# Token stage of an audio tower: the first depthwise tap on ScalarE, the latents' split one iteration earlier, and another order on four queues

## The chip, the cores and the metric

The kernel runs on one core of a Trainium2 chip. The metric is the device time of one execution in microseconds (us); the figure that is compared is the median over several runs.

## The reference

Only the first of three stages is touched: a token stage, then attention, then a mixture of low-rank experts. The token stage and the start of attention, cut to what matters:

```python
h = conv1d(x, conv_in_w, pad=3)                       # x (16, 64, 2048) -> (16, 128, 2048), 7 taps
h = gelu(groupnorm1(h, gn1_w, gn1_b))                 # one mean and variance per batch element
h = conv1d(h, dw_w, stride=2, pad=2, groups=128) + dw_b   # depthwise, 5 taps -> (16, 128, 1024)
h = gelu(groupnorm1(conv1d(h, pw_w), gn2_w, gn2_b))   # pointwise 128x128
t = layernorm(h)
q_c = rmsnorm(t @ w_qa, g_qa)                         # 384 latents per token
kv = t @ w_kva; k_c = rmsnorm(kv[..., :128], g_kva)   # 128 latents, and 64 rotary columns
k_rope = rope(kv[..., 128:])
```

Everything is float32 in the reference. The kernel splits an operand into a high and a low float16 part and adds three products (high x high, high x low, low x high).

## The kernel before, in words

`token_phase` works on one batch element b at a time, 128 channels on the partitions. `pipeline` (L65) calls each engine's own `body(i, p, ok)` with i from -1 to 20; `ok(lag)` says whether batch element i - lag exists, so that one iteration works on several elements at different steps. AHEAD = -1 is the loading and splitting of x, 0 the first conv, MID = 1 GELU 1, the depthwise taps and the pointwise matmul, HID = 2 GELU 2 and the layer norm's statistics, PROJ = 3 the normalised hidden row, its turning and the projection, TAIL = 4 the latents' scales and high parts, LOW = 5 their low parts. Each engine has one queue and goes through its body in the order written; semaphores join them. A full iteration is one in which all of these exist.

What each queue does in an iteration, in order:

- **TensorE**: conv chunk 0 (12 matmuls, L561), the averaging of the statistics over the partitions (`stat_ps`, L599), conv chunks 1 to 3, `project` (48 matmuls, L582 and L583, which wait for the turned `ht`), `pointwise` (L570, waits for the five taps, `dw_step`).
- **VectorE**: copy of the averages to `s` (L490); low part of the hidden row `hid2` (L412); low parts of the latents, `latents_low`; `take_latents` (L453 to L458); statistics of y, chunk 0; `add_rotary`; chunk 1; the five `tap`s (L437 for the first, L441 for the other four); `bn_stats` and `bn_aggr` of resid (L513, L519); `reciprocal` of the latents' scales `rinv` (L523, waits for GpSimd's `rms_step`); statistics of y, chunks 2 and 3; `mean_and_square` of y (ready: `st1_ready`); statistics of the pointwise result (L536) and its `mean_and_square` (`st2_ready`).
- **ScalarE**: `hid` (L271, waits for the layer norm, `ln_step`) and its high part (L275); copies of conv results to y (L261), with the high part of the next x (`x_high`, L255) behind the first; GELU 1 (L288, waits for `gn_step`); GELU 2 (L296); the latents' high parts (L305 to L307, wait for `rinv_done`); the two squares with their sums (L314, L317, wait for the projection).
- **GpSimd**: `group_norms` (eleven small instructions, L347 to L357, waits for `s`); `x_low`, the low part of the next x (L335, 128x2054); `latent_scales` (seven small instructions, L366 to L372, waits for the squares); `layer_norm` (eight, L382 to L389, waits for `bn3_step`). In a profile the last instruction of each chain stands on its last line.
- **SP**: the turning of `hid2` (L202), the turning of the latents and of kc (L206, L209), the load of the x after next (L195, waits for both parts of x).

The lines on which order and waits hang, on VectorE:

```python
                if ok(MID):
                    for k in range(DW_TAPS):
                        tap(i - MID, k)
                ...
                if ok(TAIL):
                    b = i - TAIL
                    dve.wait_ge(rms_step, b * RMS_STEPS + RMS_STEPS)
                    dve.reciprocal(rinv[:, :], nrm[:, :]).then_inc(rinv_done, 1)
```

and on GpSimd, whose code is the same before and after:

```python
                if ok(MID) or ok(HID):
                    group_norms(i)
                if ok(AHEAD) and i >= 0:
                    x_low(i - AHEAD)
                if ok(TAIL):
                    latent_scales(i - TAIL)
                if ok(HID):
                    layer_norm(i - HID)
```

Of the kernel before, what the change touches and what calls it, by code (L numbers as in the profile page):

```python
# [18 lines left out]
ALU = mybir.AluOpType  # L19
# [5 lines left out]
XW = T + 2 * PAD  # L25
PAIRS = (TAPS + 1) // 2
D = T // 2
# [81 lines left out]
def token_phase(nc, keep, raw_loaded, x_d, wc_d, wqk_d, pw_d, rows_d, params_d, consts_d, heads_d):  # L109

    AHEAD, MID, HID, PROJ, TAIL, LOW = -1, 1, 2, 3, 4, 5
    LAST = B - 1
    with ExitStack() as ctx:
# [64 lines left out]
        lags = list(range(AHEAD, LOW + 1))  # L180
# [9 lines left out]
        def _(sp):  # L190
# [6 lines left out]
            def body(i, p, ok):  # L197
# [5 lines left out]
                if ok(LOW):  # L203
                    b = i - LOW
# [6 lines left out]
                if ok(-2) and i >= -1:  # L211
                    sp.wait_ge(x_hi, i + 2)
                    sp.wait_ge(x_lo, i + 2)
                    load(i + 2, 0, XW, x_loaded)
# [17 lines left out]
            pipeline(sp, body, -1, lags, LOW)  # L232
# [4 lines left out]
        def _(act):  # L237
# [27 lines left out]

            def body(i, p, ok):
                if ok(PROJ):
# [17 lines left out]
                if ok(MID):  # L285
# [23 lines left out]
                if ok(PROJ):  # L309
                    b = i - PROJ  # L310
                    act.wait_ge(proj_done, b + 1)
                    need(act, rms_step, b * RMS_STEPS, B * RMS_STEPS)
                    need(act, ss_done, b * 2, 2 * B)
                    act.activation(junk[:, :], q_ps[:, 0:QR], ACT.Square, scale=UN * QR ** -0.5,  # L314
                                   accum_out=ss[:, 0:1]).then_inc(ss_done, 1)
                    act.wait_ge(ss_done, b * 2 + 1)
                    act.activation(junk[:, 0:KVR], kv_ps[:, 0:KVR], ACT.Square, scale=UN * KVR ** -0.5,  # L317
                                   accum_out=ss[:, 1:2]).then_inc(ss_done, 1)

            act.wait_ge(zeroed, ZEROED)  # L320
            pipeline(act, body, -1, lags, LOW)

        @block.gpsimd
        def _(pool):
# [79 lines left out]
            pipeline(pool, body, -1, lags, LOW)  # L404

        @block.vector
        def _(dve):
# [24 lines left out]
            def tap(b, k):  # L432

                if k == 0:
                    dve.wait_ge(gelu1_done, b + 1)
                    need(dve, pw_done, b * 2, 2 * B)
# [992 lines left out]
```

## Time and profile before

| what | value |
|---|---|
| median of three runs | 2041.67 us (2041.35 to 2043.67) |
| profiled execution | 2044.69 us |
| its span | 2042.9 us, mean granted TensorE clock 0.969 |
| TensorE matmul, share of the span | 93% |
| VectorE | 65% |
| ScalarE | 38% |
| GpSimd | 15% |

The time of a run is that of the whole launch; the span is what the profiler saw between the first and the last instruction, so the profiled execution has 1.8 us around its span. The profiled execution is a run of its own and need not lie at the median. In the rows further below, times are us from the span's start, PE is TensorE, DVE VectorE, ACT ScalarE, POOL GpSimd, SPq the DMA queue of SP. Buffer numbers are left out of names (g for g1, y for y1_0 and y1_1, c for c12, lat for lat2). `x4` is a count of like instructions merged into one row, whose length is then that of all. What stands in brackets is how long the engine sat idle before, and who ended that.

### The profile page before, as it was taken

The numbers are of one execution on the slowest core, as the hardware profiler recorded it, in microseconds if no ns is written. First come the engines' busy times: TensorE is split into PE (matmuls) and PEld (weight loads), VectorE is DVE, ScalarE is ACT, GpSimd is POOL, SyncE is SP. The second block draws the span as 40 slices with busy tenths as digits, with TensorE's granted clock in tenths as the row PEclk, the third lists the DMA queues.
The fourth block names the chain that finished last, engine by engine and source line by source line (L and its number), as shares of the span: only waits on it lengthen the run. The fifth ranks groups of instructions, "written<-read, shape, count | busy, mean of one in ns | idle before, by whom it ended". The sixth has DMA issues, their size and how long they took to land. (4 is left out here: it accounts for less than half of the span.)

```text
span 2042.9 us, 32412 instructions
## 1 busy us (share of the span) xinstructions
PE 1892.5 (93%) x11538; PEld 1029.6 (50%) x11538; DVE 1321.2 (65%) x2742; ACT 773.2 (38%) x2020; POOL 308.4 (15%) x596
## 2 busy tenths in 40 slices
PE   4898898559999999999999999999999999859999
PEld 2344444335555555555555555555555555425554
DVE  4678777436666666666666666666666666555554
ACT  3454554233333334433333433333343333332221
POOL 2376675300000000000000000000000000033332
PEclk9899999679999999999999999999999999979999
DMA  5244342332222322232222222223222222243332
GB/s 143 52 86 96 81 95 65 76 91 51 58 58 59 76 56 53 58 76 59 58 58 55 73 58 58 58 58 75 55 55 58 40 39 39 39 138 80 80 82 73
DMA packets 305609, 138.87 MB, mean 68 GB/s; under 512 B 295088, under 2 KB 295344, under 8 KB 303408
## 3 DMA queue, kind: packets, MB, share of 16 engines
q1 hardware_dynamic: 301136, 108.35, 24.8%
q10 hardware_dynamic: 4320, 28.51, 4.0%
q8 instruction: 92, 1.51, 0.3%
q14 instruction: 61, 0.50, 0.1%
HBM read 56.07 MB, written 8.39 MB: 32 GB/s over the span
## 5 line engine op out<-in xcount | busy, mean ns | idle before, releaser
L1031 PE MATMUL out_ps<-m_h,ot_h 128*128 128x512 f16 x1024 | 389.4, 380 | 1.7 <-DVE ot_l L835 1.7
L1032 PE MATMUL out_ps<-m_l,ot_h 128*128 128x512 f16 x1024 | 389.0, 380 | 0.0
L1033 PE MATMUL out_ps<-m_h,ot_l 128*128 128x512 f16 x1024 | 388.9, 380 | 0.0
L756 ACT ACTIVATE qp_h<-qp_ps 128x512 f16<-128x512 f32 x126 | 75.3, 597 | 492.6 <-PE qp_ps L966 492.6
L812 ACT ACTIVATE prob<-s_ps,nmx 128x128 f32<-128x128 f32 x512 | 181.3, 366 | 207.3 <-DVE nmx L905 207.3
L885 DVE SCALAR_TENSOR_TENSOR resid<-out_ps,resid 128x512 f32<-128x512 f32 x256 | 176.1, 688 | 97.1 <-PE out_ps L1033 97.1
L835 DVE SCALAR_TENSOR_TENSOR qp_l<-qp_ps,qp_h 128x512 f16<-128x512 f32 x126 | 87.2, 692 | 234.5 <-ACT qp_h L756 234.5
L1221 POOL MEMSET fpower<- 128x1 f32 x1 | 0.1, 99 | 1392.4 <-POOLq L674 1392.4
L966 PE MATMUL qp_ps<-lat,wp_h 128*128 128x512 f16 x756 | 205.6, 381 | 0.0
L1033 PEld LDWEIGHTS out_ps<-m_h,ot_l 128*128 128x128 f16 x1024 | 100.4, 98 | 121.6 <-issue 1.4
L1031 PEld LDWEIGHTS out_ps<-m_h,ot_h 128*128 128x128 f16 x1024 | 100.5, 98 | 110.5 <-DVE ot_l L835 2.7
L1032 PEld LDWEIGHTS out_ps<-m_l,ot_h 128*128 128x128 f16 x1024 | 100.5, 98 | 107.7 <-issue 0.8
L982 PE MATMUL rope_ps<-wr_h,lat 128*128 128x256 f16 x768 | 127.8, 276 | 0.0
L966 PEld LDWEIGHTS qp_ps<-lat,wp_h 128*128 128x128 f16 x756 | 74.4, 98 | 90.9 <-issue 2.3
L835 DVE SCALAR_TENSOR_TENSOR halves<-prob,halves 128x512 f16<-128x512 f32 x128 | 88.6, 692 | 46.5 <-ACT halves L756 46.5
L756 ACT ACTIVATE halves<-prob 128x512 f16<-128x512 f32 x128 | 80.8, 631 | 84.5 <-DVE prob L911 84.5
L812 ACT ACTIVATION_READ_ACCUMULATOR prob<-s_ps,nmx 128x1 f32 x512 | 103.8, 203 | 0.0
L966 PE MATMUL qp_ps<-lat,wp_l 128*128 128x512 f16 x378 | 102.6, 381 | 0.0
L835 DVE SCALAR_TENSOR_TENSOR ot_l<-av_ps,ot_h 128x512 f16<-128x512 f32 x128 | 88.4, 690 | 21.3 <-ACT ot_h L756 17.8
L582 PE MATMUL q_ps<-wqk_h,ht 128*128 128x384 f16 x256 | 78.7, 342 | 24.5 <-DMA ht<-hid_hl 24.5
L1334 PE MATMUL fout<-wb_h,fht_h 128*128 128x512 f16 x256 | 97.3, 380 | 0.0
L1334 PE MATMUL fout<-wb_l,fht_h 128*128 128x512 f16 x256 | 97.3, 380 | 0.0
(217 smaller groups left out, 3861.3 us busy)
## 6 DMA issues: line engine op xcount, KB each, us to landing
wide<-heads_in ACTq DMA_DIRECT2D x30, 928.0 KB, 4.7
wide<-x_in SPq DMA_DIRECT2D x30, 512.0 KB, 6.5
tower_out<-result SPq DMA_DIRECT2D x16, 512.0 KB, 2.6
stage<-wb_in SPq DMA_DIRECT2D x8, 512.0 KB, 8.3
resid<-wqk_in SPq DMA_DIRECT2D x1, 2304.0 KB, 11.6
zt<-z SPq DMA_TRANSPOSE x128, 2.4
turned<-halves SPq DMA_TRANSPOSE x128, 3.0
wide<-heads_in SPq DMA_DIRECT2D x2, 928.0 KB, 4.6
```

What stands on the lines that cost most here:

```text
L582: pe.matmul(q_ps[:, 0:QR], lhs, w[:, k, 0:QR], start=first, stop=end)
L756: act.activation(out, src, ACT.Copy, scale=scale).then_inc(done, 1)
L812: act.activation(prob[:, h, :], s_ps[:, h * P:(h + 1) * P], ACT.Exp, bias=nmx[:, h:h + 1], scale=EXP_SCALE, accum_out=rsum[:, h:h + 1]).th ...
L835: dve.scalar_tensor_tensor(out=out, in0=src, scalar=scale, in1=high, op0=ALU.mult, op1=ALU.subtract).then_inc(done, 1)
L885: dve.scalar_tensor_tensor(out=resid[:, at], in0=out_ps[hf][:, :], scalar=1.0 / (O_S * M_S), in1=resid[:, at], op0=ALU.mult, op1=ALU.add). ...
L966: last = pe.matmul(bank[:, :], w[:, bass.ds(side, 1), k, j, :].rearrange("p a n -> p (a n)"), q[:, k, bass.ds(tok, CHUNK)], start=n == 0, ...
L982: last = pe.matmul(rope_ps[:, 0:HEADS * RD], q[:, k, bass.ds(tok + j * P, P)], w[:, bass.ds(side, 1), k, :].rearrange("p a n -> p (a n)"), ...
L1031: pe.matmul(out_ps[hf][:, :], ot_h[:, h, :], m_h[:, at], start=h == 0, stop=False)
L1032: pe.matmul(out_ps[hf][:, :], ot_h[:, h, :], m_l[:, at], start=False, stop=False)
L1033: last = pe.matmul(out_ps[hf][:, :], ot_l[:, h, :], m_h[:, at], start=False, stop=h == HEADS - 1)
L1221: pool.memset(power[:, :], -0.5).then_inc(powered, 1)
L1334: pe.matmul(out_ps[p][hf][:, :], h[p][:, k, :], w[:, k, hf * CHUNK:(hf + 1) * CHUNK], start=k == 0 and n == 0, stop=False)
```

## The change

- Tap 0 of the depthwise conv, with its bias, moves from VectorE (`tensor_scalar`) to ScalarE (`activation` Identity with scale and bias), right behind GELU 1. Taps 1 to 4 stay.
- `reciprocal` moves from behind bn3 to between taps 2 and 3.
- LOW is gone: the latents' low parts are made at the end of the iteration in which their high parts are made. The stage has one iteration less.
- On VectorE the low part of hid stands behind the statistics of y's chunk 0 (for i < 16; from then on in front of `take_latents`); the statistics of y's chunks 2 and 3 stand in front of those of resid, and the statistics of the pointwise result in front of y's `mean_and_square`.
- On ScalarE the squares of the last iterations (batch elements 13 to 15) stand behind hid of the iteration after.
- On SP the load of x stands in front of the latents' turnings.
- The low part of x stays on GpSimd, in its place.

The diff, cut to its core:

```diff
-    AHEAD, MID, HID, PROJ, TAIL, LOW = -1, 1, 2, 3, 4, 5
+    AHEAD, MID, HID, PROJ, TAIL = -1, 1, 2, 3, 4
...
@@ ScalarE @@
+                if ok(TAIL) and i - TAIL + PROJ >= B:
+                    squares(i - TAIL)
                 if i == 0:
...
                     act.activation(g1[:, DW_PAD:DW_PAD + T], y1[1 - p][:, :], ACT.Gelu, bias=c12[:, 1:2],
                                    scale=c12[:, 0:1]).then_inc(gelu1_done, 1)
+                    b = i - MID
+                    act.wait_ge(gelu1_done, b + 1)
+                    need(act, pw_done, b * 2, 2 * B)
+                    act.activation(dw[:, :], g1[:, 0:2 * D:2], ACT.Identity, bias=params[:, 5:6],
+                                   scale=params[:, 0:1]).then_inc(dw_step, 1)
...
+                if ok(PROJ) and i < B:
+                    squares(i - PROJ)
@@ VectorE @@
-                if ok(PROJ):
-                    b = i - PROJ
-                    dve.wait_ge(hid_hi, b + 1)
-                    need(dve, hid_turned, b * 16, B * 16)
-                    low(hid2[:, D:2 * D], hid[:, :], LN_S, hid2[:, 0:D], hid_lo)
-                if ok(LOW):
-                    latents_low(i - LOW)
+                if ok(PROJ) and i >= B:
+                    hid_low(i - PROJ)
                 if ok(TAIL):
                     take_latents(i - TAIL)
                 if ok(0):
                     stats1(i, p, 0)
+                if ok(PROJ) and i < B:
+                    hid_low(i - PROJ)
                 if ok(TAIL):
                     add_rotary(i - TAIL)
                 if ok(0):
                     stats1(i, p, 1)
-                if ok(MID):
-                    for k in range(DW_TAPS):
+                for k in range(1, DW_TAPS):
+                    if ok(MID):
                         tap(i - MID, k)
+                    if ok(TAIL) and k == 2:
+                        dve.wait_ge(rms_step, (i - TAIL) * RMS_STEPS + RMS_STEPS)
+                        dve.reciprocal(rinv[:, :], nrm[:, :]).then_inc(rinv_done, 1)
+                if ok(0):
+                    stats1(i, p, 2)
+                    stats1(i, p, 3)
                 if ok(HID):
...
+                if ok(TAIL):
+                    latents_low(i - TAIL)
@@ SP @@
+                if ok(-2) and i >= -1:
+                    sp.wait_ge(x_hi, i + 2)
+                    sp.wait_ge(x_lo, i + 2)
+                    load(i + 2, 0, XW, x_loaded)
-                if ok(LOW):
-                    b = i - LOW
+                if ok(TAIL):
+                    b = i - TAIL
```

VectorE's queue in a full iteration before, from the first tap to the copy of `s` (the names are the buffers'; bn3 and st3 belong to the layer norm):

```order
L437 TENSOR_SCALAR dw<-g1,params 128x1024 [waits pw_done,gelu1_done]
L441 SCALAR_TENSOR_TENSOR dw<-g1,params,dw 128x1024 [waits dw_step] x4
L513 BN_STATS bn3<-resid 128x6 [waits gelu2_done]
L513 BN_STATS bn3<-resid 128x6
L519 BN_AGGR st3<-bn3 128x2 [waits bn3_step,ln_step]
L523 RECIPROCAL rinv<-nrm 128x2 [waits rms_step]
L421 BN_STATS bn1<-y1_0 128x6 [waits y1_copied] x2
L428 BN_AGGR st<-bn1 128x2 [waits bn1_done,stat_done]
L429 SCALAR_TENSOR_TENSOR st<-st 128x1 [waits st1_ready]
L536 BN_STATS bn2<-pw_ps0 128x6 [waits pw_done]
L536 BN_STATS bn2<-pw_ps1 128x6 [waits pw_done]
```

The same place after the change (its lines are numbered by the changed file):

```order
L442 SCALAR_TENSOR_TENSOR dw<-g1,params,dw 128x1024 [waits dw_step] x2
L514 RECIPROCAL rinv<-nrm 128x2 [waits rms_step]
L442 SCALAR_TENSOR_TENSOR dw<-g1,params,dw 128x1024 [waits dw_step] x2
L429 BN_STATS bn1<-y1_0 128x6 [waits y1_copied] x2
L522 BN_STATS bn3<-resid 128x6 [waits gelu2_done]
L522 BN_STATS bn3<-resid 128x6
L528 BN_AGGR st3<-bn3 128x2 [waits bn3_step,ln_step]
L533 BN_STATS bn2<-pw_ps0 128x6 [waits pw_done]
L533 BN_STATS bn2<-pw_ps1 128x6 [waits pw_done]
L436 BN_AGGR st<-bn1 128x2 [waits bn1_done,stat_done]
L437 SCALAR_TENSOR_TENSOR st<-st 128x1 [waits st1_ready]
```

The first tap has left the queue, the reciprocal with its wait for GpSimd stands in front of half of the taps, and the statistics are in another order.

ScalarE's queue after the change, from the high part of the next x to the copy behind the second GELU's:

```order
L254 ACTIVATE wide1<-wide0 128x2054 [waits conv_done,x_loaded]
L260 ACTIVATE y1_1<-conv_ps2 128x512 [waits conv_done]
L299 ACTIVATE g1<-y1_0,c12 128x2048 [waits dw_step,gn_step]
L304 ACTIVATE dw<-g1,params 128x1024 [waits pw_done,gelu1_done]
L260 ACTIVATE y1_1<-conv_ps0 128x512 [waits conv_done]
L312 ACTIVATE resid<-pw_ps0,c12 128x512 [waits gn_step]
L312 ACTIVATE resid<-pw_ps1,c12 128x512
L260 ACTIVATE y1_1<-conv_ps1 128x512 [waits conv_done]
```

Its fourth row is new; before, the copy of y followed GELU 1 at once.

## Rows read from the trace of the kernel before

**Rows 1.** Busy time of each engine in two stretches of the token stage.
```profile
core 0: us, PE busy (x) PEld busy (x) DVE busy (x) ACT busy (x) POOL busy (x), PEclk, DMA share, GB/s
99.69:337.56 237.87, 210.67 (x1124) 109.68 (x1122) 185.98 (x338) 126.35 (x189) 166.36 (x298) 0.97 0.41 87
337.56:420.70 83.14, 43.10 (x239) 25.84 (x236) 40.79 (x97) 26.62 (x50) 30.08 (x92) 0.75 0.29 61
```

**Rows 2.** Timeline of VectorE, one full iteration: start, length, engine, line, instruction, idle before.
```profile
236.88 2.16 DVE L437 TENSOR_SCALAR dw<-g,params 128x1024 f32<-128x1024 f32 x1 [1.99 <-ACT g L288]
239.07 5.25 DVE L441 SCALAR_TENSOR_TENSOR dw<-g,params,dw 128x1024 f32<-128x1024 f32 x4
244.23 1.28 DVE L513 BATCH_NORM_STATS2 bn<-resid 128x6 f32<-128x512 f32 x2
...
245.81 0.11 DVE L523 RECIPROCAL rinv<-nrm 128x2 f32<-128x2 f32 x1
...
250.14 0.16 DVE L490 COPY s<-stat_ps 128x4 f32<-128x4 f32 x1 [0.49 <-PE stat_ps L599]
...
252.72 0.61 DVE L412 SCALAR_TENSOR_TENSOR lat<-q_g,rinv,lat 128x384 f16<-128x384 f32 x1
```

**Rows 3.** Timeline of GpSimd, the same iteration.
```profile
229.12 0.19 POOL L347 TENSOR_TENSOR msq<-s 128x2 f32<-128x2 f32 x1 [1.31 <-DVE s L490]
...
234.67 3.82 POOL L335 TENSOR_TENSOR x_l<-wide 128x2054 f16<-128x2054 f32 x1
...
239.30 1.63 POOL L367 TENSOR_TENSOR ry<-rv,half 128x2 f32<-128x2 f32 x1 [0.18 <-POOL rv L366]
...
246.11 0.23 POOL L382 TENSOR_SCALAR lv<-st 128x1 f32<-128x1 f32 x1 [0.98 <-DVE st L519]
...
248.99 0.19 POOL L389 TENSOR_TENSOR lc<-lm,ly 128x1 f32<-128x1 f32 x1 [0.18 <-POOL ly L388]
250.51 0.20 POOL L347 TENSOR_TENSOR msq<-s 128x2 f32<-128x2 f32 x1 [1.33 <-DVE s L490]
```

**Rows 4.** Timeline of ScalarE, the same iteration.
```profile
234.74 2.10 ACT L288 ACTIVATE g<-y,c 128x2048 f32<-128x2048 f32 x1 [1.79 <-POOL c L357]
```

**Rows 5.** Timeline of all engines, the second iteration.
```profile
39.18 4.07 POOL L335 TENSOR_TENSOR x_l<-wide 128x2054 f16<-128x2054 f32 x1 [3.56 <-ACT wide L255]
...
40.57 3.90 DVE L412 SCALAR_TENSOR_TENSOR wqk_l<-resid,wqk_h 128x1152 f16<-128x1152 f32 x1 [0.36 <-ACT wqk_h L242]
...
44.39 0.80 DVE L437 TENSOR_SCALAR dw<-g,params 128x1024 f32<-128x1024 f32 x1
```

**Rows 6.** Timeline of GpSimd, the latents' scales of the last batch.
```profile
411.24 0.21 POOL L366 TENSOR_SCALAR rv<-ss 128x2 f32<-128x2 f32 x1 [13.00 <-ACT junk L317]
411.63 0.71 POOL L367 TENSOR_TENSOR ry<-rv,half 128x2 f32<-128x2 f32 x1 [0.18 <-POOL rv L366]
...
414.05 0.19 POOL L372 TENSOR_SCALAR nrm<-nrm 128x2 f32<-128x2 f32 x1 [0.20 <-POOL nrm L371]
```

**Rows 7.** Timeline of TensorE, the same iteration and one of four with a slow pointwise matmul.
```profile
235.48 1.02 PE L561 MATMUL conv_ps<-x_l,wc_h 128*128 128x512 f16 x4
...
244.37 1.98 PE L570 MATMUL pw_ps<-dw,pw 128*128 128x512 f32 x4 [1.90 <-DVE dw L441]
...
330.76 3.35 PE L570 MATMUL pw_ps<-dw,pw 128*128 128x512 f32 x4 [1.98 <-DVE dw L441]
```

**Rows 8.** Timeline of all engines, the drained end of the stage.
```profile
388.19 0.19 POOL L389 TENSOR_TENSOR lc<-lm,ly 128x1 f32<-128x1 f32 x1 [0.18 <-POOL ly L388]
...
392.74 0.49 ACT L314 ACTIVATE junk<-q_ps 128x384 f16<-128x384 f32 x1 [6.10 <-PE kv_ps L583]
...
393.62 1.23 ACT L271 ACTIVATE hid<-resid,lc,ly 128x1024 f32<-128x1024 f32 x1
...
397.22 1.86 SPq L202 DMA_TRANSPOSE ht<-hid_hl  x1
...
401.72 0.48 PE L582 MATMUL q_ps<-wqk_h,ht 128*128 128x384 f16 x1 [9.02 <-DMA ht<-hid_hl]
```

More of the change, by code:

```diff
@@ L179, in token_phase @@
         HEAD = 2 * CHUNK + 8
-        lags = list(range(AHEAD, LOW + 1))
+        lags = list(range(AHEAD, TAIL + 1))
         block = ctx.enter_context(nc.Block())
@@ L264, in copy_y1, with squares @@
                     weights_high("wqk", QUARTERS[c])
+            def squares(b):
+                act.wait_ge(proj_done, b + 1)
+                need(act, rms_step, b * RMS_STEPS, B * RMS_STEPS)
+                need(act, ss_done, b * 2, 2 * B)
+                act.activation(junk[:, :], q_ps[:, 0:QR], ACT.Square, scale=UN * QR ** -0.5,
+                               accum_out=ss[:, 0:1]).then_inc(ss_done, 1)
+                act.wait_ge(ss_done, b * 2 + 1)
+                act.activation(junk[:, 0:KVR], kv_ps[:, 0:KVR], ACT.Square, scale=UN * KVR ** -0.5,
+                               accum_out=ss[:, 1:2]).then_inc(ss_done, 1)
             def body(i, p, ok):
@@ L432, in tap, with hid_low @@
             def tap(b, k):
-                if k == 0:
-                    dve.wait_ge(gelu1_done, b + 1)
-                    need(dve, pw_done, b * 2, 2 * B)
-                    dve.tensor_scalar(dw[:, :], g1[:, 0:2 * D:2], params[:, 0:1], params[:, 5:6],
-                                      ALU.mult, ALU.add).then_inc(dw_step, 1)
-                else:
-                    dve.wait_ge(dw_step, b * DW_TAPS + k)
-                    dve.scalar_tensor_tensor(out=dw[:, :], in0=g1[:, k:k + 2 * D - 1:2],
-                                             scalar=params[:, k:k + 1], in1=dw[:, :],
-                                             op0=ALU.mult, op1=ALU.add).then_inc(dw_step, 1)
+                dve.wait_ge(dw_step, b * DW_TAPS + k)
+                dve.scalar_tensor_tensor(out=dw[:, :], in0=g1[:, k:k + 2 * D - 1:2],
+                                         scalar=params[:, k:k + 1], in1=dw[:, :],
+                                         op0=ALU.mult, op1=ALU.add).then_inc(dw_step, 1)
+            def hid_low(b):
+                dve.wait_ge(hid_hi, b + 1)
+                need(dve, hid_turned, b * 16, B * 16)
+                low(hid2[:, D:2 * D], hid[:, :], LN_S, hid2[:, 0:D], hid_lo)
             def take_latents(b):
@@ L519, in body @@
                     dve.bn_aggr(st3[:, :], bn3[:, :, :]).then_inc(bn3_step, 1)
-                if ok(TAIL):
-                    b = i - TAIL
-                    dve.wait_ge(rms_step, b * RMS_STEPS + RMS_STEPS)
-                    dve.reciprocal(rinv[:, :], nrm[:, :]).then_inc(rinv_done, 1)
+                if ok(MID):
+                    b = i - MID
+                    for hf in range(2):
+                        dve.wait_ge(pw_done, b * 2 + (hf + 1))
+                        dve.bn_stats(bn2[:, hf, :], pw_ps[hf][:, :]).then_inc(bn2_done, 1)
                 if ok(0):
-                    stats1(i, p, 2)
-                    stats1(i, p, 3)
                     waits = [(bn1_done, i * 4 + 4)]
@@ L532, in body @@
                 if ok(MID):
-                    b = i - MID
-                    for hf in range(2):
-                        dve.wait_ge(pw_done, b * 2 + (hf + 1))
-                        dve.bn_stats(bn2[:, hf, :], pw_ps[hf][:, :]).then_inc(bn2_done, 1)
                     wait_apart(dve, dve_passed, (bn2_done, b * 2 + 2), (stat_done, i))
                     mean_and_square(st2_ready, b, st[:, 2:4], bn2[:, :, :])
+                if ok(TAIL):
+                    latents_low(i - TAIL)
             dve.wait_ge(zeroed, ZEROED)
             dve.wait_ge(w_loaded["params"], 16)
-            pipeline(dve, body, -1, lags, LOW)
+            pipeline(dve, body, -1, lags, TAIL)
         @block.tensor
```

22 lines of the change are left out of this document (4 added, 18 removed).

## Prediction

> **What bounds the kernel now.** I read the windows first [rows 1]. The token stage runs to 420.70 us of a span of 2042.9, and only that stage is touched. Its full iterations (i = 4 to 14, the 11 that load, convolve, scale and project at once) take 237.87 us, 21.62 each. VectorE is busy 185.98 of them and TensorE 210.67 (its granted clock 0.97), so neither is full by itself: something hands on. To see what, I followed one iteration through the timelines of VectorE and GpSimd [rows 2, 3], from GpSimd's first group-norm instruction at 229.12 to the next at 250.51: 21.39 us, in three pieces.
>
> - A, 9.37 us: the small group-norm instructions to 234.67, then the low half of x, 3.82 us, to 238.49. ScalarE's GELU starts when the group norm is done and ends at 236.84 [rows 4].
> - B, 5.83 us: tap 0 on VectorE starts at 236.88 but takes 2.16 us, to 239.04, though it needs 0.80 when GpSimd is idle; then four taps of 1.28 to 244.32.
> - C, 6.19 us: `bn_stats`, the moments of both group norms (249.65), the averaging matmul, the copy of `s` at 250.14, and GpSimd's start.
>
> All of it is one chain, without slack. GpSimd's other work hangs beside it: the seven instructions of the latents' scales after the low half, of which VectorE's reciprocal at 245.81 did not wait, and the layer norm, 246.11 to 249.18.
>
> The other thing to see is that GpSimd and VectorE hold each other up. A split of wqk on VectorE that started at 40.57 beside the low half of x (39.18 to 43.25) took 3.90 us and ended at 44.47 [rows 5]: it stood until 43.25 and ended 1.22 later. The other way round, GpSimd's pow at 239.30 took 1.63 us and ended at 240.93, 0.57 after tap 1 had ended [rows 3]; with VectorE idle it takes 0.71, and the seven instructions of the scales 3.00 (411.24 to 414.24) [rows 6].
>
> **The change, part by part.**
>
> *Tap 0 on ScalarE.* VectorE loses 2.19 us (236.88 to 239.07) an iteration. ScalarE gains one Identity of 128x1024; nearest rows are 1.23 for the same form without a stride (hid, at 393.62) [rows 8] and 2.10 for 2048 elements [rows 4]; I take 1.25 and keep 2.10 as the end. GELU ends 7.72 into the cycle, so tap 0 is done at 9.0, before the low half of x (9.3). Tap 1 reads two operands from SBUF as the wqk split did, so it cannot go before the low half is over: it ends 1.20 after that where tap 1 ended 240.36, 1.87 after it. The tap is worth 0.65 us, not 2.19, and ScalarE's price is covered by the low half; at 2.10 it would miss by 0.5. The low half itself does not move: its code on GpSimd is the same, and so are its order and its length (3.82 to 4.1).
>
> The Trainium skill ("SBUF — State Buffer", SBUF: two separate sides) says that whichever of the two engines starts first keeps the pair for its whole instruction and the other is blocked fully. By that rule tap 1 would begin from nothing at the end of the low half and end 1.28 after it, where the wqk row shows 1.22; the sum would be 1 us higher.
>
> *The reciprocal between taps 2 and 3.* This is the term that decides. `rinv` is wanted 4.4 us earlier than before, and the reciprocal is a wait in the middle of VectorE's queue: taps 3 and 4, the pointwise matmul, all `bn_stats` after them, the layer norm and the next group norm stand behind it. GpSimd computes the scales after the low half. Counted from the end of the low half: its first small instruction is held by tap 1 to 1.20, the pow by tap 2 to 2.48 and ends 0.57 later, at 3.05; VectorE now stands, so the five left go unheld in 1.90 (pow's end at 412.34 to 414.24 [rows 6]), to 4.95; the reciprocal with its handing over 0.20; taps 3 and 4 2.56. B becomes **7.71 instead of 5.83**, +1.88 us, with a wait of about 2.4 us that was not there. Bounds: +0.0 if tap 1 and 2 do not hold GpSimd (3.1 for the scales, 0.2, 2.56), +3.2 if one more hold of a tap's length (1.28) falls into the five.
>
> *Stats 2, 3 before bn3, latents' low parts at the end.* The two `bn_stats` of y go ahead of those of resid, 1.2 us, so the layer norm's input is ready 2.8 after the last tap instead of 1.6. GpSimd then needs 0.2 + 3.08 (246.11 to 249.18) + 0.2 [rows 3]: the next group norm can start at 6.2. Other path: the moments, 5.33 after the last tap now, come some 0.4 sooner (no reciprocal, and waits on the instruction before are filled by others), at 4.9; then the low parts of the latents (three instructions, the first 0.61 at 252.72; about 1.1 together [rows 2]) stand ahead of the copy of `s`, to 6.0, and 0.36 of handing over: 6.35. They also hold the layer norm's last instructions, 0 to 1.0; I take 0.2. C is 6.4, +0.2. Where they stood before, behind the copy, they cost nothing, and the space left there is idle now.
>
> *Low part of hid behind the first stats.* As long as hid's own making (1.23 for 128x1024 [rows 8]), it holds one of GpSimd's group-norm instructions, as before, only later in their chain. A stays at 9.37; bounds −1.2 (no hold) and +0.3.
>
> *Queues.* The transpose of hid is issued some 2 us later in the cycle, since ScalarE makes hid when the layer norm is done and its low part comes after the first stats. From issue (397.22) to the projection's first matmul (401.72) is 4.5 us [rows 8], so the projection starts near 9.0, 1.6 us after the last conv. It takes 6.0 (from the last conv's end at 236.50 to 1.90 before the pointwise matmul at 244.37 [rows 7]) and ends at 15.0; the pointwise matmul waits for the last tap at 17.1. Covered. If that cover of 2.1 us went, each iteration would pay what is over. SP now loads x ahead of the latents' transposes: it waits for the low half anyway, and the landing has a whole iteration. Free.
>
> *First and last iterations.* i = 2 and 3 have no reciprocal: they gain 0.65 each, −1.3. At the end, ScalarE stood idle 6.10 us for the projection of b = 14 and only then made hid of b = 15 (393.62), whose layer norm was done at 388.38 [rows 8]. Now the squares come behind it: up to 5.2 us. But from i = 15 each iteration hands on lateness: +0.6 for i = 15 (tap 0 there 1.25 against 0.80), +2.0 for i = 16 (the layer norm is done at the cycle's start instead of 1.3 before, the latents' low parts stand ahead of the copy), and bn3 of b = 15 now waits for the reciprocal, +1.3. Net −1.3.
>
> **Sum.** Per full iteration 1.87 + 0.2 = +2.07, 11 times: +22.8. The mean of 21.62 stands 0.23 above the iteration that I followed: in 4 of the 11 TensorE's clock is down at the pointwise matmul (3.35 us for it at 330.76, 1.98 at 244.37 [rows 7]) and the averaging matmul is late. In the longer C about half of these 2.5 us is covered: −1.2. With −1.3 and −1.3: **+19.0 us**. The profiled execution, 2044.69, would be 2063.7. It stood 3.0 above the median of the runs, 2041.67, and a median is what is forecast: **2060.7 us**, slower by 0.9%. What lies within 0.2% (4 us) a measurement of this kernel can't tell from no change.
>
> **The rivals.**
>
> *1. GpSimd is not held.* Its small instructions slip in beside taps 1 and 2. The point that decides is the end of the scales: at 3.1 us after the low half the reciprocal costs nothing, since tap 2 ends at 2.5 and the gain of 0.65 pays the rest. The loop stays at 21.6, and the ends give −1.3 and, with nothing handed on late, −5.2: 2035.2, faster. For it: VectorE idles longer in the new order, and at 411.24 the same chain ran unheld [rows 6]. Against: rows 3, in every full iteration. 0.10. If the last part gives less, about 2039: no change, 0.05.
> The Trainium skill ("Perfetto Trace Analysis", Optimizing Scalar/DVE Operations) says that where VectorE is saturated, giving some work to ScalarE can make sense. Here VectorE is at 78%, so the rule's condition is not met; read as 2.19 us less on one engine and 1.25 more on another, it would give −0.94 an iteration, some −10 us with nothing else, 2031.
>
> *2. TensorE's clock stays low.* There are now two gaps a cycle (1.6 and 1.9 us). Should the clock be down at 1.2 GHz for half of the projection, that takes 3.0 more and ends at 18.0, 0.9 after the last tap, and the pointwise matmul 1.4 more; with the first conv behind it slow in part, the averaging matmul comes some 1.5 later than C allows: 11 x 1.5 more, 2077. For it: a granted clock of 0.75 in the drained part, where TensorE waits [rows 1]. Against: 0.97 in the full iterations, with one gap of 1.90 already in each. 0.08.
>
> *3. The wait is longer than forecast*, since the reciprocal stands behind one more hold (B +3.2): 2075; or part of it is hidden (B +1.0): 2051. Both are the forecast's own mechanism, within its 0.77. That the change would do nothing is not a rival: the program orders differ in every iteration.
>
> **How the numbers follow.** 0.77 for the forecast (2051 to 2069), 0.10 for rival 1 faster, 0.05 no change, 0.08 for rival 2. The range 2048 to 2069 leaves out rival 1, rival 2 and a small part of the forecast's upper end. Faster 0.11, same 0.05, slower 0.84.
>
> **What would show it.** In the changed profile: full iterations of 23.4 to 23.8 us between copies of `s`; a new wait "VectorE reciprocal on GpSimd nrm", 2.0 to 2.8 us long, 11 times; tap 0 on ScalarE 1.2 to 1.3; tap 1 of about 1.3 to 1.6 that ends 1.2 after the low half; the scales' chain 4.9 long; no ScalarE idle before hid of b = 15. Wrong would be: a reciprocal without a wait (then rival 1), tap 1 that runs beside the low half, or TensorE with a clock under 0.9 in 100 to 350 us (rival 2).

## Result and profile after

The changed kernel takes **2054.99 us** (median of 4 runs, 2054.52 to 2056.96). Beside it the kernel before took 2042.31 (4 runs); the ratio is 1.0065, with a 95% interval from 1.0053 to 1.0077. It is slower by 12.7 us. Forecast were 2060.7 and a range of 2048 to 2069: right in sign, inside the range, 5.7 us too high; as a difference, 12.7 us where 19.0 were forecast. The profiled execution took 2054.52 us, 1.8 more than its span.

The page of the changed kernel, its head:

```profile
span 2052.7 us, 32412 instructions
## 1 busy us (share of the span) xinstructions
PE 1895.9 (92%) x11538; PEld 1031.7 (50%) x11538; DVE 1288.9 (63%) x2726; ACT 795.2 (39%) x2036; POOL 287.4 (14%) x596
```

The windows, cut 0.36 us behind the same copies of `s` as [rows 1] (the 11 full iterations, then the drained end):

```profile
core 0: us, PE busy (x) PEld busy (x) DVE busy (x) ACT busy (x) POOL busy (x), PEclk, DMA share, GB/s
94.77:348.90 254.13, 215.76 (x1126) 112.39 (x1124) 162.08 (x332) 141.06 (x198) 147.65 (x298) 0.96 0.38 78
348.90:431.00 82.10, 43.28 (x237) 25.92 (x235) 37.87 (x91) 31.28 (x53) 27.27 (x94) 0.76 0.33 73
```

The full iterations take 254.13 us instead of 237.87, although VectorE is busy 24 us less (162.08 against 185.98). It lost work and gained idle time. The timeline of VectorE, the same full iteration as [rows 2]:

```profile
237.57 1.23 DVE L420 SCALAR_TENSOR_TENSOR hid_hl<-hid,hid_hl 128x1024 f16<-128x1024 f32 x1
...
242.74 2.68 DVE L442 SCALAR_TENSOR_TENSOR dw<-g,params,dw 128x1024 f32<-128x1024 f32 x2 [2.78 <-ACT dw L304]
247.93 0.17 DVE L514 RECIPROCAL rinv<-nrm 128x2 f32<-128x2 f32 x1 [2.51 <-POOL nrm L380]
248.01 2.58 DVE L442 SCALAR_TENSOR_TENSOR dw<-g,params,dw 128x1024 f32<-128x1024 f32 x2
250.51 1.28 DVE L429 BATCH_NORM_STATS2 bn<-y 128x6 f32<-128x512 f32 x2
...
256.24 0.15 DVE L496 COPY s<-stat_ps 128x4 f32<-128x4 f32 x1
```

GpSimd over the same time, which answers to [rows 3]:

```profile
234.12 0.19 POOL L355 TENSOR_TENSOR msq<-s 128x2 f32<-128x2 f32 x1
...
237.91 0.95 POOL L364 TENSOR_TENSOR msq<-s,c 128x2 f32<-128x2 f32 x1 [0.18 <-POOL c L363]
...
239.19 3.82 POOL L343 TENSOR_TENSOR x_l<-wide 128x2054 f16<-128x2054 f32 x1
243.10 1.07 POOL L374 TENSOR_SCALAR rv<-ss 128x2 f32<-128x2 f32 x1
244.35 1.64 POOL L375 TENSOR_TENSOR ry<-rv,half 128x2 f32<-128x2 f32 x1 [0.18 <-POOL rv L374]
246.17 0.20 POOL L376 TENSOR_TENSOR rv<-rv,ry 128x2 f32<-128x2 f32 x1 [0.18 <-POOL ry L375]
...
247.70 0.19 POOL L380 TENSOR_SCALAR nrm<-nrm 128x2 f32<-128x2 f32 x1 [0.19 <-POOL nrm L379]
...
255.32 0.59 POOL L394 TENSOR_TENSOR lt<-lt,lv 128x1 f32<-128x1 f32 x1 [0.18 <-POOL lt L393]
...
256.93 0.19 POOL L397 TENSOR_TENSOR lc<-lm,ly 128x1 f32<-128x1 f32 x1 [0.18 <-POOL ly L396]
257.15 0.19 POOL L355 TENSOR_TENSOR msq<-s 128x2 f32<-128x2 f32 x1
```

Taps 1 and 2 run until 245.42 and hold the first two instructions of the scales (1.07 and 1.64 us instead of 0.21 and 0.71). Then VectorE stands for 2.51 us until the last of the seven, at 247.89, releases the reciprocal. The last rows show a second thing: the next group norm, at 257.15, starts with no idle time right behind the layer norm, while the copy of `s` had ended at 256.39; before, GpSimd stood there for 1.33 us and waited for the copy [rows 3]. The waits of the token stage show the reciprocal's as a new line (14 times; the 11 in the full iterations are 2.50 to 2.52 us each), and the tap's new place (engine, what it waits for, total, times, longest):

```profile
DVE dw L442 <- ACT dw L304: 47.9, 16, 5.3
DVE rinv L514 <- POOL nrm L380: 35.1, 14, 3.7
```

From the same views come the pieces of one iteration, as the prediction cuts it: A from GpSimd's first group-norm instruction to the end of the low half of x, B from there to the end of the last tap, C to the next first instruction. The last column is the distance between copies of `s`, the mean of the 11 full iterations. The first three columns and their sum are of one iteration in the middle of the stage. The kernels below the row of the forecast are told of in the next section.

| kernel | A | B | C | sum | mean of 11 |
|---|---|---|---|---|---|
| before | 9.37 | 5.83 | 6.19 | 21.39 | 21.62 |
| changed | 8.89 | 7.58 | 6.56 | 23.03 | 23.10 |
| forecast | 9.37 | 7.71 | 6.4 | 23.48 | 23.58 |
| tap on ScalarE alone | 9.35 | 5.05 | 6.19 | 20.59 | 20.69 |
| reciprocal back | 8.89 | 5.04 | 6.25 | 20.18 | 20.48 |
| reciprocal behind tap 4 | 8.89 | 5.05 | 7.95 | 21.89 | 21.99 |
| reciprocal behind tap 3 | 8.89 | 6.70 | 6.55 | 22.14 | 22.22 |
| tap 0 back | 8.88 | 7.47 | 6.55 | 22.90 | 23.00 |
| low parts behind the copy | 8.95 | 7.57 | 6.40 | 22.92 | 22.99 |
| best | 9.31 | 5.03 | 5.66 | 20.00 | 20.06 |

One iteration is not the mean: the low half of x takes 3.8 and 4.1 us by turns, and the holds in A and the end of C differ between iterations. As means of the 11, A, B and C are 9.37, 5.83 and 6.43 before and 8.99, 7.58 and 6.54 in the changed kernel. So the 1.48 us an iteration are made of −0.37, +1.74 and +0.11 (rounded).

### The profile page after: what moved, and what is told of

It reads as the page before. It is cut to its first block and busy times, and to the rows that moved or that the text cites. A ratio compares the mean times of both kernels' runs of the same rounds, so it can differ in the third digit from the quotient of the medians.

```text
span 2052.7 us, 32412 instructions
## 1 busy us (share of the span) xinstructions
PE 1895.9 (92%) x11538; PEld 1031.7 (50%) x11538; DVE 1288.9 (63%) x2726; ACT 795.2 (39%) x2036; POOL 287.4 (14%) x596
## 5 line engine op out<-in xcount | busy, mean ns | idle before, releaser
L588 PE MATMUL q_ps<-wqk_h,ht 128*128 128x384 f16 x256 | 85.3, 365 | 55.1 <-DMA ht<-hid_hl 55.1
L442 DVE SCALAR_TENSOR_TENSOR dw<-g,params,dw 128x1024 f32<-128x1024 f32 x64 | 84.5, 1320 | 49.2 <-ACT dw L304 47.9
```

The lines of the kernel that those rows point to most:

```text
L442: dve.scalar_tensor_tensor(out=dw[:, :], in0=g1[:, k:k + 2 * D - 1:2], scalar=params[:, k:k + 1], in1=dw[:, :], op0=ALU.mult, op1=ALU.add) ...
L588: pe.matmul(q_ps[:, 0:QR], lhs, w[:, k, 0:QR], start=first, stop=end)
```

## Experiments

The theory: the reciprocal in the middle of the taps makes VectorE wait for GpSimd's scales, and that costs some 2.6 us in each of 11 iterations, while the rest of the change gains. The rivals: something else of the change costs (the low parts ahead of the copy, the order of statistics, the squares), or the tap on ScalarE does. Each ratio is to runs of the kernel before on the same chip.

**The reciprocal goes back behind bn3**, all else as changed.

```diff
-                    if ok(TAIL) and k == 2:
-                        dve.wait_ge(rms_step, (i - TAIL) * RMS_STEPS + RMS_STEPS)
-                        dve.reciprocal(rinv[:, :], nrm[:, :]).then_inc(rinv_done, 1)
...
                     dve.bn_aggr(st3[:, :], bn3[:, :, :]).then_inc(bn3_step, 1)
+                if ok(TAIL):
+                    dve.wait_ge(rms_step, (i - TAIL) * RMS_STEPS + RMS_STEPS)
+                    dve.reciprocal(rinv[:, :], nrm[:, :]).then_inc(rinv_done, 1)
```

> The changed kernel with the reciprocal moved back behind the statistics of resid; all else as changed. Theory W (the wait in the middle of the taps is what costs): the wait of 2.5 us on nrm goes, GpSimd's chain is held by all taps again, and a full cycle falls from 23.1 to 20.6 to 21.0 us (9.0 to the end of the low half of x, 5.0 of taps, 6.6 behind them, some loss to the projection, which now ends after the last tap): 11 cycles of -2.2, so some 2031, ratio to the kernel before 0.993 to 0.997. Rival O (the new order of the statistics and of the latents' low parts is what costs): the time stays at 2050 to 2055.

Measured: 2025.98 us, ratio 0.9930 (0.9917 to 0.9944), faster than the 2031 that were expected. The reversal is worth 2.62 us an iteration, and the rest of the change is a gain of 14 us. Its VectorE and GpSimd:

```profile
227.47 5.32 DVE L442 SCALAR_TENSOR_TENSOR dw<-g,params,dw 128x1024 f32<-128x1024 f32 x4 [2.78 <-ACT dw L304]
...
231.71 1.14 POOL L377 TENSOR_TENSOR rt<-rv,ry 128x2 f32<-128x2 f32 x1 [0.18 <-POOL rv L376]
...
233.81 0.19 POOL L380 TENSOR_SCALAR nrm<-nrm 128x2 f32<-128x2 f32 x1 [0.20 <-POOL nrm L379]
...
235.48 0.11 DVE L528 RECIPROCAL rinv<-nrm 128x2 f32<-128x2 f32 x1
```

The four taps run on end, the scales are held longer (they end 6.25 us after the low half instead of 4.88), and nobody waits: the reciprocal comes 1.5 us later still. Ten of the 11 iterations take 20.34 in the mean. In the last one the projection falls on a stretch at the lower clock, takes 7.70 us instead of 6.04, and the iteration takes 21.83.

**The reciprocal alone**, put between taps 2 and 3 of the kernel before (tap 0 stays on VectorE).

```diff
+                    if ok(TAIL) and k == 2:
+                        dve.wait_ge(rms_step, (i - TAIL) * RMS_STEPS + RMS_STEPS)
+                        dve.reciprocal(rinv[:, :], nrm[:, :]).then_inc(rinv_done, 1)
```

> The kernel before with one edit: the reciprocal and its wait between taps 2 and 3. Theory W: GpSimd's first three small instructions are held by taps 0, 1 and 2, the rest runs unheld; reciprocal 4.85 us after the low half of x, last tap at 7.45 instead of 5.83: +1.6 us in each of 11 cycles, +15 to +20 in all, 2057 to 2062, ratio 1.007 to 1.010. Rival O: at most +3.

Measured: 2062.04 us, ratio 1.0112 (1.0097 to 1.0128), at the upper end of what was expected. The wait is 1.61 us and the last tap ends 7.47 us after the low half, where 7.45 was thought, but the distance between copies of `s` is 23.63, 2.01 more than before: 1.64 in B, and 0.47 in C, which was not forecast (A takes 0.11 back). From 214 us on it alternates (25.21, then 22.70 from 239.25 to 261.95). The timeline of VectorE and TensorE in a long one:

```profile
228.86 0.17 DVE L511 RECIPROCAL rinv<-nrm 128x2 f32<-128x2 f32 x1 [1.61 <-POOL nrm L372]
...
231.59 3.78 PE L569 MATMUL pw_ps<-dw,pw 128*128 128x512 f32 x4 [3.91 <-DVE dw L441]
...
239.25 0.16 DVE L490 COPY s<-stat_ps 128x4 f32<-128x4 f32 x1 [2.46 <-PE stat_ps L598]
```

Here the projection is over early, TensorE stands for 3.91 us before the pointwise matmul, and this then takes 3.78 us, about twice the 1.98 of [rows 7]; the copy waits 2.46 for the averages instead of 0.49. The granted clock over the full iterations is 0.93, against 0.97 before. The wait of VectorE is handed on as a second price at TensorE: C is 8.09 in this iteration and 6.13 in the next, where the four matmuls take 1.98. In the changed kernel that part is covered, as point 5 below shows.

**The tap alone**: tap 0 on ScalarE in the kernel before.

```diff
+                    act.activation(dw[:, :], g1[:, 0:2 * D:2], ACT.Identity, bias=params[:, 5:6],
+                                   scale=params[:, 0:1]).then_inc(dw_step, 1)
...
-                    for k in range(DW_TAPS):
+                    for k in range(1, DW_TAPS):
```

> The kernel before with one edit: tap 0 on ScalarE behind GELU 1. Theory L (the low half of x on GpSimd holds the first tap whichever it is): tap 1 ends 1.14 us after the low half instead of 1.87, so -0.7 us a cycle, 11 to 13 cycles, +0.4 in the two iterations without a low half: -7 to -9 in all, 2033 to 2035, ratio 0.995 to 0.9965. Rival (ScalarE's tap is simply taken off VectorE, 2.19 less and 1.30 more in the chain, no hold): -0.9 a cycle and tap 1 starting before the low half ends: -10 or more; rival 2 (nothing gained, the tap was covered): 0.

Measured: 2030.49 us, ratio 0.9952 (0.9939 to 0.9966), 0.93 us an iteration. B is 0.79 shorter. C is 0.24 shorter in the mean: TensorE's clock is 1.00 in this stretch, and no iteration has a late averaging matmul. A is 0.09 longer in the mean:

```profile
95.90:323.50 227.60, 204.86 (x1124) 107.82 (x1123) 162.66 (x328) 140.30 (x199) 162.98 (x297) 1.00 0.43 91
```

**The latents' low parts behind the copy**, one iteration later, as before the change. SP's old order (load of x last) came back with it, so the two are not told apart.

```diff
-                if ok(TAIL):
-                    latents_low(i - TAIL)
...
+                if ok(LOW):
+                    latents_low(i - LOW)
                 if ok(TAIL):
                     take_latents(i - TAIL)
```

> The changed kernel with the latents' low parts one iteration later again, behind the copy of s, and SP's order as before. Theory (they stand ahead of the copy and hold the layer norm's last instructions): the piece behind the taps falls from 6.56 to about 6.2 us, -0.35 a cycle, -3 to -5 in all against the changed kernel, 2050 to 2052, ratio 1.004 to 1.005. Rival O: this is where the loss is, -10 or more. Rival 3: nothing, since the layer norm itself sets the next group norm.

Measured: 2050.97 us, ratio 1.0054 (1.0040 to 1.0068). Its interval overlaps that of the changed kernel, so the time alone does not settle it. The trace gives 0.11 us an iteration (22.99 against 23.10), a third of the 0.35 that were expected: small, and not where the 12.7 us come from. The low parts hold GpSimd in either place: ahead of the copy it is the layer norm's fifth and sixth instruction (0.59 and 0.27 us), behind it the seventh and eighth (0.50 and 0.29), 0.19 each unheld.

**The changed kernel again**, on the chip of the two runs that follow and of the best version.

> The changed kernel once more, on the same chip as the three runs beside it, as their yardstick. Ratio to the kernel before 1.0053 to 1.0077, as measured first.

Measured: 2055.44 us, ratio 1.0064 (1.0050 to 1.0077).

**The scales ahead of the low half of x** on GpSimd, so that the reciprocal finds them ready.

```diff
-                if ok(AHEAD) and i >= 0:
-                    x_low(i - AHEAD)
                 if ok(TAIL):
                     latent_scales(i - TAIL)
+                if ok(AHEAD) and i >= 0:
+                    x_low(i - AHEAD)
```

> The changed kernel with the latents' scales ahead of the low half of x on GpSimd. Theory G (GpSimd's share of the cycle, group norm 5.1 + low half 3.9 + scales, sets when taps 3 and 4 can run, and the wait on nrm is only where it shows): the scales run unheld in 3.0 and the reciprocal waits no longer, but the low half then ends 12.0 us into the cycle and holds tap 1 until then; last tap at 17.0 instead of 16.5, a cycle of 23.4 to 23.7: 2058 to 2062, ratio 1.008 to 1.010. Theory W' (the reciprocal's wait alone costs): about the time of the run with the reciprocal moved back, 2026 to 2030.

Measured: 2062.76 us, ratio 1.0108 (1.0091 to 1.0125), just above what theory G gave. The seven instructions take 3.01 us unheld and the reciprocal has no wait, but the low half ends 12.35 after the iteration's start, and no tap gets past it:

```profile
247.83 3.82 POOL L343 TENSOR_TENSOR x_l<-wide 128x2054 f16<-128x2054 f32 x1
248.15 5.90 DVE L442 SCALAR_TENSOR_TENSOR dw<-g,params,dw 128x1024 f32<-128x1024 f32 x2 [3.13 <-ACT dw L304]
253.97 0.16 DVE L514 RECIPROCAL rinv<-nrm 128x2 f32<-128x2 f32 x1
```

Two taps take 5.90 instead of 2.56. The two lock each other out, in whichever order: a reciprocal so early has to be paid for once, as a wait or as a hold.

**The squares of batch elements 13 to 15 at their old place.**

```diff
-                if ok(TAIL) and i - TAIL + PROJ >= B:
-                    squares(i - TAIL)
...
-                if ok(PROJ) and i < B:
+                if ok(PROJ):
```

> The changed kernel with the two squares of batch elements 13 to 15 at their old place, at the end of the iteration. Theory D (moving them gave the drained end back what the rest of the change costs there): the end of the stage is 2 to 5 us longer, ratio 1.0075 to 1.009 where the changed kernel has 1.0065. Rival: nothing, because the projection of b = 15 waits for that of b = 14 and for its transposes anyway.

Measured: 2060.10 us, ratio 1.0088 (1.0074 to 1.0102). hid of element 15 starts at 408.11 instead of 404.07, and attention's first matmul at 434.71 instead of 431.44. The move gains 3.3 us by the trace, and 4.7 by the medians (2055.44 for the changed kernel beside it).

**The reciprocal behind tap 3, and behind tap 4**, ahead of all statistics (`k == 3` and `k == 4` in place of `k == 2`).

> The changed kernel with the reciprocal one tap later, between taps 3 and 4. Theory H (the scales' instructions on GpSimd are held by each tap that runs, and the reciprocal stalls the rest): tap 3 ends 3.8 us after the low half of x and holds the instruction behind the pow until then; the three behind that run unheld and end near 5.3; the reciprocal 5.5, the last tap 6.8 after the low half instead of 7.6. 0.8 us an iteration less than the changed kernel, cycle 22.3, 11 x 0.8 = 9 us: 2044 to 2048, 1.001 to 1.004 of the kernel before. Theory F (only the place of bn3 and of the low parts costs): no difference from the changed kernel, 2055.

> The changed kernel with the reciprocal right behind tap 4, ahead of all statistics. Theory H: the four taps end 5.1 us after the low half; the chain of scales has one more held instruction, ends near 6.2, and the reciprocal waits 1.1 and ends at 6.4; the statistics behind it start there instead of at 7.6. Cycle 21.9, 11 x 1.2 = 13 us less than the changed kernel: 2040 to 2044, 0.999 to 1.002 of the kernel before; slower than the same kernel with the reciprocal behind bn3 (2026 in an earlier run, 0.993), where the wait is gone. Theory F: 2055.

Measured: behind tap 3 2046.78 us, ratio 1.0018 (1.0008 to 1.0028); behind tap 4 2043.01, ratio 1.0001 (0.9991 to 1.0011). Both lie in what the theory gave, with 10 runs each. First behind tap 3, then behind tap 4:

```profile
243.92 0.17 DVE L514 RECIPROCAL rinv<-nrm 128x2 f32<-128x2 f32 x1 [1.62 <-POOL nrm L380]
244.01 1.27 DVE L442 SCALAR_TENSOR_TENSOR dw<-g,params,dw 128x1024 f32<-128x1024 f32 x1
```

```profile
237.14 5.32 DVE L442 SCALAR_TENSOR_TENSOR dw<-g,params,dw 128x1024 f32<-128x1024 f32 x4 [2.79 <-ACT dw L304]
...
243.70 0.17 DVE L514 RECIPROCAL rinv<-nrm 128x2 f32<-128x2 f32 x1 [1.24 <-POOL nrm L380]
```

With nothing changed but the place of one instruction of 0.17 us, the wait goes 2.51, 1.62, 1.24, none, and the iteration 23.10, 22.22, 21.99, 20.48. Each tap that goes ahead holds GpSimd once more (0.62 instead of 0.20 us, then 1.14 instead of 0.20), so a tap of 1.28 us buys 0.9 and then 0.4 of wait. The last step, behind the statistics, takes off 1.5: the rest of the wait, the reciprocal and its handing over.

**Tap 0 back on VectorE**, the reciprocal where the change puts it (the tap as in the kernel before, the rest as changed).

> The changed kernel with tap 0 back on VectorE; the reciprocal stays between taps 2 and 3. Theory H (GpSimd's scales are held by the taps, and the wait sets the cycle): with tap 0 back the taps end and so the holds come 0.65 us later, so the scales and the reciprocal come 0.65 later, but the wait of the reciprocal stays near 1.6 to 2.5 us; 11 x 0.65 is +7 us on the changed kernel: 2062 to 2066, 1.009 to 1.012 of the kernel before. Theory F (the scales have their own time, 5 us after the low half, whatever VectorE does): the wait only gets shorter by 0.65, and the time is that of the changed kernel, 2055.

Measured: 2053.63 us, ratio 1.0073 (1.0056 to 1.0090). Theory H, my own, fell here, and F held: what gained 9 us in the kernel before gains nothing that can be measured in the changed one. VectorE and GpSimd from the end of the low half, 244.53:

```profile
242.91 2.16 DVE L438 TENSOR_SCALAR dw<-g,params 128x1024 f32<-128x1024 f32 x1 [1.44 <-ACT g L299]
...
244.61 0.54 POOL L369 TENSOR_SCALAR rv<-ss 128x2 f32<-128x2 f32 x1
...
245.33 1.64 POOL L370 TENSOR_TENSOR ry<-rv,half 128x2 f32<-128x2 f32 x1 [0.18 <-POOL rv L369]
...
249.10 0.19 POOL L375 TENSOR_SCALAR nrm<-nrm 128x2 f32<-128x2 f32 x1 [0.20 <-POOL nrm L374]
249.33 0.17 DVE L517 RECIPROCAL rinv<-nrm 128x2 f32<-128x2 f32 x1 [1.61 <-POOL nrm L375]
```

The scales end 4.76 us after the low half here, 4.88 in the changed kernel. The taps lie some 0.7 later, so the first instruction of the scales is held less (0.54 instead of 1.07), and one behind the pow a little more (L371, 0.62 instead of 0.20). The last tap hangs on the scales, so the earlier tap only makes the wait longer (2.51 instead of 1.61).

**Next to no low half of x**: 8 of its 2054 columns are computed and the rest is left out, so that GpSimd has no long instruction.

```diff
+            pool.memset(x_l[1][:, :], 0.0)
...
-                pool.tensor_tensor(x_l[p][:, :], x_f[:, :], x_h[p][:, :], ALU.subtract).then_inc(x_lo, 1)
+                pool.tensor_tensor(x_l[p][:, 0:8], x_f[:, 0:8], x_h[p][:, 0:8], ALU.subtract).then_inc(x_lo, 1)
```

> The changed kernel in which the low half of x is computed for 8 of its 2054 columns only and the rest of that tile holds zeros or stale halves; all other instructions are there. Theory H: with the low half away the scales run from 5.1 us after the cycle's start and are done near 8.5, before tap 2 ends; the reciprocal loses its wait, tap 1 follows tap 0 at 9.0 unheld, the last tap ends near 14.0 instead of 16.5. The cycle goes from 23.1 to about 20.5 us, unless the projection, which then ends last, holds TensorE; 2025 to 2030, 0.991 to 0.994 of the kernel before. Rival (the wait comes of the latents' squares or of VectorE's order, not of GpSimd's load): cycle over 22.5 us and a time over 2045.

Measured: 2021.85 us, ratio 0.9911 (0.9895 to 0.9928), below what was expected; the distance between copies is 20.41. GpSimd's last instruction of the scales and VectorE:

```profile
223.22 0.19 POOL L381 TENSOR_SCALAR nrm<-nrm 128x2 f32<-128x2 f32 x1 [0.20 <-POOL nrm L380]
...
223.68 2.61 DVE L443 SCALAR_TENSOR_TENSOR dw<-g,params,dw 128x1024 f32<-128x1024 f32 x2 [3.13 <-ACT dw L304]
...
226.20 0.16 DVE L515 RECIPROCAL rinv<-nrm 128x2 f32<-128x2 f32 x1
```

The scales are done before tap 1 starts, and the reciprocal between taps 2 and 3 costs nothing. What it waits for in the changed kernel is GpSimd's load, not the projection and not the squares.

**The best version**: the changed kernel with the reciprocal behind bn3, bn3 ahead of the statistics of y's chunks 2 and 3 again, and the latents' low parts behind the copy (with SP's old order).

> What the runs so far point to: the changed kernel with the reciprocal behind the statistics of resid, these ahead of the statistics of y's chunks 2 and 3, and the latents' low parts behind the copy of s in the next iteration. The layer norm's input is ready 1.2 us sooner and nothing stands ahead of the copy of s: the piece behind the last tap falls from 6.25 to 5.8, a cycle from 20.3 to 19.8 or 19.9: 4 to 6 us faster than the run with the reciprocal back, 2020 to 2022, ratio 0.990 to 0.992. Rival: TensorE has become the bound (it has 18.7 us of work a cycle and stands 2.0 for the transposes): no gain, 0.993.

Measured: 2020.07 us, ratio 0.9892 (0.9876 to 0.9907): 22.8 us under the kernel before, and faster than the run with the reciprocal back (0.9930). C is 5.66, since the layer norm starts at once and ends before the copy of `s`, for which GpSimd now stands 0.79 us. But A is 9.31 instead of 8.89, and the cycle 20.06 where 19.8 or 19.9 were expected: behind the copy the latents' low parts hold the first two instructions of the group norm (0.39 and 0.29 us, 0.20 unheld), and the low part of hid now holds its seventh for 1.08 us, where it held its tenth for 0.95.

## Why the prediction was right, and where its sizes were off

1. **The reciprocal.** This term held. B was forecast at 7.71 and is 7.58; the wait was forecast at about 2.4 and is 2.51; the end of the scales at 4.95 after the low half and is 4.88, with the two held instructions and the five unheld ones as reckoned. Set against the 5.04 that B takes with the reciprocal back, the wait and the reciprocal cost 2.54, and the whole iteration 2.62. Rival 1, GpSimd not held, is out: with taps 1 and 2 ahead, the same chain that takes 3.00 unheld takes 4.80. The 0.13 that B was put too high are 1.5 us in the 11 iterations.
2. **The tap on ScalarE.** It takes 1.30 us (forecast 1.25; hid, without a stride, takes 1.24), and it is covered by the low half. Tap 1 ends 1.08 us after the low half in each of the 11 iterations, where 1.20 was taken from the wqk row of [rows 5]:

```profile
242.74 1.36 DVE L442 SCALAR_TENSOR_TENSOR dw<-g,params,dw 128x1024 f32<-128x1024 f32 x1 [2.78 <-ACT dw L304]
```

 By the rule cited from the Trainium skill ("SBUF — State Buffer", SBUF: two separate sides) it would be 1.28; so 0.20 us of the tap lies beside the low half, and the rule is nearly right. Worth 0.65 the tap was only where it stands alone (0.79 in B). In the changed kernel it is worth nothing in the loop, since the scales set the last tap's time. The prediction wrote the 0.65 down as a gain; its sum did not lean on it, because B was reckoned from the end of the low half.
3. **Low part of hid, piece A.** This is the term that was mis-sized most: "A stays at 9.37". It is 8.89 in the iteration followed and 8.99 in the mean, and 0.37 in 11 iterations is 4.1 us of the 5.3 by which the loop was forecast too high; it is most of why the full iterations take 23.10 us and not the 23.4 to 23.8 that were named as a sign. The low part does hold one instruction, but another one, and less of it. Before, it held the pow. VectorE and GpSimd:

```profile
230.21 1.23 DVE L412 SCALAR_TENSOR_TENSOR hid_hl<-hid,hid_hl 128x1024 f16<-128x1024 f32 x1 [1.29 <-ACT hid_hl L275]
230.31 1.71 POOL L350 TENSOR_TENSOR gy<-gv,half 128x2 f32<-128x2 f32 x1 [0.18 <-POOL gv L349]
```

 When the pow came up at 230.31, 1.13 us of the low part were left; unheld it takes 0.73 (235.30 in the changed kernel), so the hold cost 0.98. In the changed kernel the multiply of L364 comes up at 237.91, when 0.89 of the low part (237.57 to 238.80) are left, and takes 0.95 instead of 0.19: 0.76. In the kernel before two more of the chain were held a little (0.29 and 0.34 instead of 0.20; the first by the latents' low part of kc, which ended at 232.42), and that makes up the rest. So the low parts behind the copy did not "cost nothing", as the prediction had it. I had written the bounds down from −1.2 and chosen the end near zero without looking at where in the chain the hold falls. No run undid this move by itself; the account is read from the traces.
4. **Statistics and low parts, piece C.** Forecast +0.2, measured +0.37 in the iteration followed. The forecast had two paths that end almost together, the layer norm at 6.2 with 0.2 of hold, and the copy of `s` at 6.0 with GpSimd behind it at 6.35. The copy starts at 256.24, 5.65 after the last tap, so this path is 0.35 shorter, and the layer norm alone sets C: it starts 2.99 after the last tap instead of 1.79, and takes 3.54 instead of 3.07, since the latents' low parts hold two of its instructions for 0.47 (0.2 was forecast). With the low parts behind the copy C is 6.40, so their place is worth 0.16; the rest is the order of the statistics, since the best version has C at 5.66 with bn3 first. With the clock, the mean of C grew by 0.11, where 0.09 was forecast: that this fits is luck, a price taken too low beside a cover taken too small.
5. **The clock.** Half of 2.5 us was forecast as covered; all of it is: no C of the 11 is longer than 6.57, where four were 6.85 before. (The mean stands 0.07 above the iteration followed because of the low half's two lengths.) TensorE does stand more often now, before the projection as well, and the granted clock is 0.96 against 0.97. But the slow stretch now falls on the projection. In 6 of the 11 iterations some of its matmuls of 384 columns take 0.53 instead of 0.33 us, and it takes 7.5 to 7.7 instead of 6.04; the windows over the projection of two iterations in a row, in the changed kernel:

```profile
243.20:250.00 6.80, 6.04 (x48) 4.28 (x48) 4.21 (x5) 3.58 (x9) 3.58 (x7) 1.00 0.70 157
266.00:272.50 6.50, 6.07 (x39) 4.20 (x40) 3.96 (x4) 3.13 (x7) 3.96 (x8) 0.74 0.73 161
```

 Even so the pointwise matmul starts at most 0.2 us after the last tap there (0.06 after it elsewhere). Rival 2 had this mechanism, and here it is hidden, since the wait for GpSimd has made room for it. The run with the reciprocal alone, and the last full iteration of the run with the reciprocal back, show what a slow stretch costs uncovered.
6. **First and last iterations.** i = 2 and 3: forecast −1.3, measured −1.7. i = 15: forecast +0.6, measured +1.87 (21.69 against 19.82), because the cover of the projection is gone there. With no x to split the reciprocal has no wait, the last tap ends at 363.29, 14.8 after the copy instead of 17.4, and the pointwise matmul starts at 365.86, behind a projection at the lower clock. I had named this cover for the full iterations and not looked it up for this one. i = 16: forecast +2.0, measured +0.53. The squares: up to 5.2 was allowed, 3.3 measured; ScalarE does not start hid of b = 15 at once, as the prediction's signs had it, but stands 3.96 us for the layer norm (404.07). From the copy of i = 15 to attention 82.90 us instead of 83.56: −0.7 against a forecast of −1.3. That these are near each other is luck: the errors at i = 15 (+1.3) and i = 16 (−1.5) cancel.

Together: 16.3 in the loop, −1.7 and −0.7 at its ends, −0.9 in the rest of the program. That is 13.0, beside 12.7 by the medians. The profiled execution of the kernel before had its second copy of `s`, that of i = 2, 3.2 us later than the changed one's (57.52 and 54.32), and 2.5 of it stood there already at the first low half of x (25.51 and 23.05), where both kernels had done the same; in the second profile of the changed kernel this copy stands at 55.75, so it differs from run to run. It is why the two spans differ by 9.8 only.

## What to carry to other kernels

Moving an instruction that waits costs what is queued behind it, not its own 0.17 us: before you make a result earlier, look up when its input is ready and put the wait where the engine would be busy until then. Work taken off an engine gains only if nothing else sets the end: the same tap gave 9 us alone and nothing behind the wait. And where two engines hold each other up, look at each place at how much of the one's instruction is left when the other comes to its own: that is what a hold costs.

## What the runs showed of the hardware

- A hold of GpSimd costs what is left of VectorE's instruction when GpSimd comes to its own, less 0.13 to 0.15 us, a pow or a plain instruction alike. That is so for all 448 small group-norm and scale instructions of GpSimd, in nine runs from 95 to 345 us, that came up while an instruction of VectorE over 1 us long ran, a tap or the low part of hid, with 0.46 to 1.19 us left of it. A plain one (0.19 to 0.24 us unheld) therefore ends 0.05 to 0.10 us after VectorE's, a pow (0.71 to 0.73) 0.56 to 0.59. The low part of hid, 1.23 us, cost 0.98 at the pow and 0.76 at the multiply because 1.13 and 0.89 us of it were left there.
- Back-to-back taps let in one of GpSimd's small instructions each: in the run with the reciprocal back, four of them (1.07, 1.64, 0.62, 1.14) end right behind a tap or, the pow, within the next one, and the chain of seven takes 6.2 instead of 3.0.
- In the run with the reciprocal alone TensorE stands 3.2 to 3.9 us before the pointwise matmul in every full iteration, where it stood 1.6 to 2.3 before. The four matmuls then take 3.78 us in three iterations, 2.5 to 3.6 in four and 1.98 in four. The length of the gap does not tell which: 3.38 was followed by 1.98 and 3.46 by 3.78. Where it was 3.78 late in the stage, C is 8.0 instead of 6.1. In the changed kernel gaps of 2.2 to 2.9 stand ahead of the projection and the slow stretch falls on it; there it costs nothing. What matters is which work the slow stretch falls on.
